# A transformer layer on one core: five engines leave one shared list of steps and each walk a table of its own

## The chip, the cores and the metric

The kernel runs on one core of one Trainium2 chip. The metric is the time of one execution on the device, in microseconds (us), the median of three runs. The core's engines run side by side, each through its own queue in order, and meet through semaphores: TensorE (PE; its weight loads are PEld), VectorE (DVE), ScalarE (ACT), GpSimd (POOL) and SyncE (SP), which here only starts DMAs. An instruction that waits holds everything behind it on its engine.

## The reference

The input is 16 sequences of 128 tokens with 256 channels. Three residual blocks follow each other, each fed by a layer norm:

```python
x = x + attn(layernorm(x))        # 16 heads with 72 latent dims, causal, keys = values = x @ latent_w + latent_b
x = x + birwkv(layernorm(x), ctx) # sigmoid(r) * (Af + Ab + e^(u+k) v) / (Bf + Bb + e^(u+k)); scans forwards and backwards in time
x = x + moe(layernorm(x))         # router over 8 experts, top 2, silu(x Wg) * (x Wu), then Wd, weighted sum
```

In the attention, q is projected per head, scores are masked and go through a softmax, the mixed latents of the 16 heads are projected by `out_w`. In the last block each token goes to its two best experts (512 hidden units each), and the two results are added with the router's weights.

## The kernel before, in words

**Steps.** The whole program is cut into named steps, such as `S.17` or `up.3.0`. One list, `STEPS`, completed by `schedule()` into `ORDER`, holds all of them. Each of the five engine programs walks that same list and does its own part of each step, or nothing. So a step can stand only at one place, and all its parts stand at that place in their engines' queues.

**Attention.** Work goes by 64 units; a unit is one sequence and four of its heads. A unit n has these steps: `S.n` (scores on PE, L743 and L750; row maximum on DVE, L1235; exponentials on ACT, L1011), `N.n` (reciprocal of the sums on DVE, L1239; the multiplication of the probabilities on POOL, L1633), `T.n` (transposition on PE, L758; copy on ACT, L1016) and `Y.n` (the product with the values on PE, L768; copy on DVE, L1250; the store by head for SP, L577). Two score banks and three probability buffers are used in turn, so `S.n` waits for the exponentials of unit n-2. The queries of two sequences are one group k: `q.k.i` projects them (PE), adds the bias (ACT, L1004) and SP moves them to another layout (L564, tile qT); unit 8k is the first to need them all. `O.b.i` projects the result of sequence b (PE, L796, and L781 for the last sequence); `add` adds it to x.

**Scans.** They lie beside the attention, for four groups g of four sequences and two channel halves k: `w1` to `w5` (DVE, L1264, L1274 and L1276 are the multiplication and the four scans), `w6`, `w7` and `wa` (POOL), `w8` (reciprocals on DVE, L1281) and `wb.g.k` (transposition on PE, L803; copy on ACT, L1044).

**Router and plan.** `x2`, `bn`, `agg`, `rs`, `nmb`, `xn`, `tx` (kind 3), `lg`, `r1` to `r4`, `ra` and `rw` choose experts and slots for a group of sequences; `lg` is L812, `r3` is L819 and L823 on PE, which waits for `r2` on DVE (L1344). `p1`, `p2` and `p3` (DVE, L1378 to L1473) plan which expert each tile of tokens takes: `p*.0` for the first five tiles after the third group, `p*.1` for the rest.

**Experts.** There are 23 tiles: 16 of 256 token slots with weights split in a high and a low part, then 7 of 128. Tile j has: `lw.j.k` (SP loads a third of its weights, 512 KB), `sw.j.k` (high part on ACT, L1076; low part on DVE, L1162), `ltk.j` (SP loads its token list, L635), `lxg.j` (POOL gathers its rows, L1690), `tg.j` (transposition on PE, L838; copies on ACT and DVE), `up.j.n`, `si`, `hd`, `sh` (gate and up products on PE, L672 or L872; silu and hidden values), `dn.j` (down product on PE, L672 or L881; weighting on ACT, L1105) and `ao.j` (POOL adds the rows into the output by an indirect DMA, L1717). `ao.j` waits until the adds of tile j-1 have landed, and the ACT part of `dn.j` waits for those of tile j-2. `gtk`, `gw` are the same loads for the first tiles, issued by POOL.

**Order.** What an engine does next is fixed by its place in `ORDER` alone. The waits are worked out from counts over `ORDER` and state what data or buffer must be ready.

## Time and profile before

| | us |
|---|---|
| median of 3 runs | 597.67 |
| lowest and highest | 597.42, 598.23 |
| span of the profiled execution | 602.4 |
| PE busy in it | 524.7 |
| DVE, ACT, POOL busy | 363.1, 329.2, 314.9 |

The profiled execution is 4.7 us longer than the median. A stretch in which PE is not busy, or busy at a granted clock below 1.00, is one in which the busiest engine does less than it could. "PEclk" is that clock as a share of 2.4 GHz; 0.50 is 1.2 GHz. Within the records, work that PE does for one step can hold a wait of its own between two matmul groups.

### The profile page before, as it was taken

The page shows a single profiled execution, that of the slowest core. Times are in us where ns is not written, and L with a number is a line of the kernel's source. Part 1 is how long each engine was busy: PE and PEld are TensorE (multiplying, and loading weights), DVE is VectorE, ACT ScalarE, POOL GpSimd, SP SyncE. Part 2 cuts the span into 40 slices and gives each one's busy share as a digit, 9 for nine tenths or more (in the row PEclk, how much of TensorE's full clock was granted, in tenths as well). Part 3 has the DMA queues.
Part 4 walks back from the last instruction along what each step waited for, and adds up shares of the span by engine and source line. Part 5 has one row for each costly group of instructions (what it writes and reads, how often), then busy time and mean ns, then how long its engine had stood idle before and what let it go on. Part 6 is the DMA issues. An engine that isn't in the chain of part 4 may idle for free.

```text
span 602.4 us, 10421 instructions
## 1 busy us (share of the span) xinstructions
PE 524.7 (87%) x3490; PEld 455.9 (76%) x3490; DVE 363.1 (60%) x749; ACT 329.2 (55%) x944; POOL 314.9 (52%) x277
## 2 busy tenths in 40 slices
...
PEclk9999999998999999999988879589999999999797
...
GB/s 189 166 3 123 58 65 101 57 72 87 57 96 102 65 59 66 105 77 70 64 26 91 111 140 226 124 96 83 280 154 287 210 238 228 235 253 358 176 27 0
DMA packets 53087, 75.65 MB, mean 126 GB/s; under 512 B 10185, under 2 KB 41674, under 8 KB 52778
## 3 DMA queue, kind: packets, MB, share of 16 engines
...
q10 hardware_dynamic: 888, 0.15, 0.1%
...
## 4 chain that ended last, share of the span: by engine, by line
PE 39%; DMA 22%; issue 12%; DVE 9%; POOL 9%; ACT 4%; SPq 3%; POOLq 1%; another core or an unknown queue 0%; ACTq 0%
DMA out<-Y,TK 14%; PE P L672 10%; PE PO L796 8%; PE P L750 6%; PE P L768 5%; DMA qT<-qP 3%; POOL out L1717 3%; PE P L758 3%; DMA zP<-ZT 2%; SPq L577 2%; POOL cxa L1690 2%; ACT EB L1011 2%; POOL xs L1676 1%; DMA arena<-wd 1%; PE P L743 1%
## 5 line engine op out<-in xcount | busy, mean ns | idle before, releaser
L1011 ACT ACTIVATE EB<-P,small 128x128 f32<-128x128 f32 x256 | 90.7, 369 | 79.3 <-DVE small L1235 60.1
L1633 POOL TENSOR_TENSOR EB<-EB,small 128x512 f32<-128x512 f32 x64 | 78.9, 1241 | 98.4 <-DVE small L1239 98.2
L672 PE MATMUL P<-GT,WF 128*128 128x256 f32 x768 | 100.8, 290 | 7.2 <-DVE GT L1162 2.6
L672 PEld LDWEIGHTS P<-GT,WF 128*128 128x128 f32 x768 | 96.4, 196 | 8.2 <-DVE GT L1162 3.1
L1717 POOL DMA_INDIRECT out<-Y,TK x39 | 67.4, 1729 | 66.3 <-DMA out<-Y,TK 28.9
L768 PE MATMUL P<-PT,V 128*72 128x512 f32 x128 | 68.7, 619 | 11.2 <-ACT PT L1016 10.1
L750 PEld LDWEIGHTS P<-KT,qT 72*128 72x128 f32 x512 | 67.7, 194 | 12.6 <-DMA qT<-qP 6.8
L750 PE MATMUL P<-KT,qT 72*128 72x128 f32 x512 | 68.9, 278 | 5.4 <-DMA qT<-qP 4.7
L796 PE MATMUL PO<-Ow,zP 128*128 128x256 f32 x270 | 71.2, 407 | 2.0 <-DMA zP<-ZT 1.9
L1250 DVE COPY ZT<-P 72x512 f32<-72x512 f32 x64 | 43.3, 677 | 45.1 <-PE P L768 42.1
L796 PEld LDWEIGHTS PO<-Ow,zP 128*128 128x128 f32 x270 | 52.9, 205 | 17.2 <-issue 10.7
L1235 DVE TENSOR_REDUCE small<-P 128x4 f32<-128x512 f32 x64 | 43.4, 678 | 27.1 <-PE P L750 25.6
L1016 ACT ACTIVATE PT<-P 128x512 f32<-128x512 f32 x64 | 38.8, 606 | 33.5 <-PE P L758 33.5
L1690 POOL DMA_INDIRECT cxa<-xd,TK x39 | 43.1, 1104 | 25.1 <-DMA TK<-xs 11.8
L672 PE MATMUL PO<-WF,HR 128*128 128x256 f32 x384 | 49.0, 284 | 4.8 <-issue 4.8
L1011 ACT ACTIVATION_READ_ACCUMULATOR EB<-P,small 128x1 f32 x256 | 52.9, 207 | 0.0
L1676 POOL DMA_INDIRECT xs<-TKS,SL x32 | 33.5, 1048 | 35.9 <-DVE TKS L1370 25.6
L672 PEld LDWEIGHTS PO<-WF,HR 128*128 128x128 f32 x384 | 47.1, 192 | 5.2 <-issue 5.2
L758 PEld LDWEIGHTS P<-ident,EB 128*128 128x128 f32 x256 | 31.6, 145 | 21.4 <-issue 11.4
L758 PE MATMUL P<-ident,EB 128*128 128x128 f32 x256 | 39.7, 278 | 3.3 <-POOL EB L1633 3.1
L1105 ACT ACTIVATE Y<-PO,TK 128x256 f32<-128x256 f32 x39 | 16.7, 470 | 45.6 <-DMA out<-Y,TK 25.4
L672 PE MATMUL P<-xnTa,Wd 128*128 128x256 f32 (+1 forms) x258 | 38.5, 303 | 2.7 <-ACT qP L1004 2.6
...
## 6 DMA issues: line engine op xcount, KB each, us to landing
...
```

The source lines that it names most:

```text
L672: r = e.matmul(o, lt(a), rt_(b), start=start and n == 0, stop=stop and n == 2, skip_group_check=skip)
L750: p = e.matmul(S[:, 128 * j:128 * j + 128], qT[k % 2][:, 4 * hq + j, c:c + 128], KT[g % 2][:, r:r + 128], start=False, stop=True, skip_gro ...
L758: p = e.transpose(PTB[:, 128 * j:128 * j + 128], EB[n % 3][:, j, :], ident[:, :])
L768: e.matmul(YB[0:L, :], V[g % 2][:, b % GB, :], PT[n % 2][:, :], start=True, stop=True).then_inc(s_Y, 1)
L796: p = e.matmul(o, zP[b // NB % 2][:, m, 128 * (b % NB):128 * (b % NB) + 128], Ow[:, m, :], start=m == 0, stop=m == NQ - 1)
L1011: e.activation(EB[i][:, j, :], S[:, 128 * j:128 * j + 128], ACT.Exp, bias=NM[i][:, j:j + 1], accum_out=SM[i][:, j:j + 1]).then_inc(s_exp, 1)
L1235: e.tensor_reduce(NM[n % 3], SB[n % 2][:, :].rearrange("p (h s) -> p h s", h=4), AX.X, ALU.max, negate=True).then_inc(s_max, 1)
L1250: e.tensor_copy(ZT[buf][:, :, c:c + 128], YB[0:L, :].rearrange("p (h t) -> p h t", h=4)).then_inc(s_z, 1)
L1633: e.tensor_tensor(EB[i][:, :, :], EB[i][:, :, :], SM[i].unsqueeze(2).broadcast_to([128, 4, 128]), ALU.mult).then_inc(s_prob, 1)
L1676: e.indirect_dma_start(xs, bass.IndirectOffsetOnAxis(ap=SL[:, g, c, b:b + 1], axis=0), TKS[:, g, c, b, :], None).then_inc(s_sc[g], 16)
L1690: e.indirect_dma_start(XG[i][:, a_, :], None, xd[0:(TN * 3 // 4, TN + 1)[phase(j)], :], bass.IndirectOffsetOnAxis(ap=TK[:, j, a_, 0:1].bit ...
L1717: e.indirect_dma_start(outr, bass.IndirectOffsetOnAxis(ap=TK[:, j, a_, 0:1].bitcast(i32), axis=0), Y[j % 2][:, a_, :], None, bounds_check= ...
```

## The change

Five tables stand beside `STEPS`: `SYNC_STEPS`, `TENSOR_STEPS`, `VECTOR_STEPS`, `SCALAR_STEPS` and `GPSIMD_STEPS`. Each engine's loop walks its own table. `ORDER` remains, and all waits are still worked out from it, so every step waits for the same events as before. Every step that has instructions on an engine is in that engine's table once. No instruction is added or removed.

```diff
+SYNC_STEPS = """
+    ctx.0 ctx.1 q.1.0 q.1.1 q.1.2 q.1.3 q.1.4 Y.1 Y.3 q.2.0 q.2.1 Y.5 Y.7 q.2.2 q.2.3 q.2.4 Y.9 ctx.2 q.3.0 q.3.1 Y.11 q.3.2 Y.13 Y.15 q.3.3 q.3.4
...
+def steps_of(table):
+
+    return [(name, *map(int, a)) for name, *a in (w.split(".") for w in table.split())]
...
-            for name, *a in ORDER:
+            for name, *a in steps_of(SYNC_STEPS):
...
-            for name, *a in ORDER:
+            for name, *a in steps_of(TENSOR_STEPS):
...
-            for s in ORDER:
+            for s in steps_of(GPSIMD_STEPS):
                 name, a = s[0], s[1:]
```

The order of the steps within one kind is kept on every engine, but for the weight parts `lw` and `sw` of neighbouring tiles. What moves is how the kinds interleave: on PE, the `q` come on average 4 steps earlier and the `Y` 2 steps later; on DVE the `w8` come on average 16 steps earlier; on SP the `ltk` 13 steps earlier and the `out` stores 12 later.

**Place 1, the end of the attention, DVE.** Lines of before are those of the profile; in the changed kernel all of them are 102 higher. L1402 to L1409 are `p3.0`; the reductions from P1 and P2 are the row maxima of units 62 and 63; the copies to ZT are `Y` steps. Before:

```order
L1235 TENSOR_REDUCE small<-P1 128x4
L1250 COPY ZT1<-P4 72x4x128
L1239 RECIPROCAL small<-small 128x4
L1402 TENSOR_TENSOR small<-small 1x40
L1403 TENSOR_TENSOR small<-small 1x40
L1404 TENSOR_REDUCE small<-small 1x5
L1405 SCALAR_TENSOR_TENSOR small<-small 1x5
L1406 TENSOR_SCALAR small<-small 1x5
L1407 TENSOR_TENSOR small<-small 1x5
L1408 TENSOR_TENSOR small<-small 1x5
L1409 CAST PI<-small 1x5
L1235 TENSOR_REDUCE small<-P2 128x4
```

After `p3.0` the maximum of unit 63 is next on DVE. Now:

```order
L1504 TENSOR_TENSOR small<-small 1x40
L1505 TENSOR_TENSOR small<-small 1x40
L1506 TENSOR_REDUCE small<-small 1x5
L1507 SCALAR_TENSOR_TENSOR small<-small 1x5
L1508 TENSOR_SCALAR small<-small 1x5
L1509 TENSOR_TENSOR small<-small 1x5
L1510 TENSOR_TENSOR small<-small 1x5
L1511 CAST PI<-small 1x5
L1352 COPY ZT1<-P4 72x4x128
L1337 TENSOR_REDUCE small<-P1 128x4
L1341 RECIPROCAL small<-small 128x4
L1352 COPY ZT0<-P4 72x4x128
```

Both maxima have moved behind `p3.0`: that of unit 62 stands between the `Y` copies of units 59 and 60, and that of unit 63 follows four rows below.

**The same place on PE.** L743 and L750 are `S`, L758 `T`, L768 `Y`, L796 and L781 `O`. Before:

```order
L743 MATMUL P2<-maskr,identr 128x512
L750 MATMUL P2<-KT1,qT1 128x128 x4
L768 MATMUL P4<-PT1,V1 72x512
L758 MATMUL P3<-ident,EB0 128x128 x4
L768 MATMUL P4<-PT0,V1 72x512
L796 MATMUL PO<-Ow,zP1 128x256 x3
L758 MATMUL P3<-ident,EB1 128x128 x4
L768 MATMUL P4<-PT1,V1 72x512
```

These are `S.63`, `Y.59`, `T.60`, `Y.60`, `O.14.0`, `T.61` and `Y.61`: the last scores stand ahead of `T.60`. Now (L860 is `T`, L870 `Y`, L898 `O`, L905 `wb`):

```order
L860 MATMUL P3<-ident,EB0 128x128 x4
L898 MATMUL PO<-Ow,zP0 128x256 x9
L870 MATMUL P4<-PT1,V1 72x512
L860 MATMUL P3<-ident,EB1 128x128 x4
L845 MATMUL P2<-maskr,identr 128x512
L852 MATMUL P2<-KT1,qT1 128x128 x4
L905 MATMUL PO<-ident,cu2 128x128 x4
L870 MATMUL P4<-PT0,V1 72x512
L860 MATMUL P3<-ident,EB2 128x128 x4
L870 MATMUL P4<-PT1,V1 72x512
```

`T.60` has moved ahead of `S.63`; the whole of `O.13` stands between `T.60` and `T.61`, and `wb.3.1` behind `S.63`.

**Place 2, the first expert tiles, PE.** `up.0.0` is the pair on P0 and P2, `up.0.1` the pair on P1 and P3; L819 and L823 are `r3.3`, L812 `lg.3`, L838 `tg`. Before:

```order
L672 MATMUL P0<-GT0,WF0 128x256 x12
L672 MATMUL P2<-GT0,WF0 128x256 x12
L690 MATMUL P5<-ident,XN 128x128 x4
L812 MATMUL P5<-small,XT3 128x8 x8
L819 MATMUL P5<-Mr,Utr 128x32
L823 MATMUL P5<-Mr,onem 128x8 x10
L672 MATMUL P1<-GT0,WF0 128x256 x12
L672 MATMUL P3<-GT0,WF0 128x256 x12
L838 MATMUL P4<-ident,cxa 128x128 x4
L672 MATMUL PO<-WF0,HR0 128x256 x24
L672 MATMUL P0<-GT1,WF1 128x256 x12
L672 MATMUL P2<-GT1,WF1 128x256 x12
```

`r3.3` stands ahead of `up.0.1`. Now (L914 is `lg`, L921 and L925 `r3`, L940 `tg`):

```order
L774 MATMUL P2<-GT0,WF0 128x256 x12
L792 MATMUL P5<-ident,XN 128x128 x2
L940 MATMUL P4<-ident,cxa 128x128 x4
L792 MATMUL P5<-ident,XN 128x128 x2
L914 MATMUL P5<-small,XT3 128x8 x8
L774 MATMUL P1<-GT0,WF0 128x256 x12
L774 MATMUL P3<-GT0,WF0 128x256 x12
L940 MATMUL P4<-ident,cxa 128x128 x4
L774 MATMUL P0<-GT1,WF1 128x256 x12
L774 MATMUL P2<-GT1,WF1 128x256 x12
L921 MATMUL P5<-Mr,Utr 128x32
L925 MATMUL P5<-Mr,onem 128x8 x10
```

`up.0.1`, `tg.2` and `up.1.0` have moved ahead of `r3.3`, and `tg.1` between the two transpositions.

**Place 3, the last expert tiles, POOL.** L1690 gathers rows (`lxg`), L1717 adds results (`ao`); the first rows here are `ao.12`. Before:

```order
L1717 DMA out<-Y0,TK 2048x256 x2
L1690 DMA cxa<-xd,TK 128x256
L1717 DMA out<-Y1,TK 2048x256 x2
L1690 DMA cxa<-xd,TK 128x256
L1717 DMA out<-Y0,TK 2048x256 x2
L1690 DMA cxa<-xd,TK 128x256
L1717 DMA out<-Y1,TK 2048x256 x2
L1690 DMA cxa<-xd,TK 128x256
L1717 DMA out<-Y0,TK 2048x256
L1690 DMA cxa<-xd,TK 128x256
```

Each gather stands behind the add of a tile five earlier. Now, from the same add (L1792 gathers, L1819 adds):

```order
L1819 DMA out<-Y0,TK 2048x256 x2
L1792 DMA cxa<-xd,TK 128x256 x3
L1819 DMA out<-Y1,TK 2048x256 x2
L1819 DMA out<-Y0,TK 2048x256 x2
L1819 DMA out<-Y1,TK 2048x256 x2
L1819 DMA out<-Y0,TK 2048x256
L1792 DMA cxa<-xd,TK 128x256 x3
L1819 DMA out<-Y1,TK 2048x256
```

The gathers of tiles 17, 18 and 19 stand in one row behind `ao.12`, and those of 20 to 22 behind `ao.16`.

## Rows read from the trace of the kernel before

**Rows 1.** The page: the granted TensorE clock in 40 slices of the span, in tenths.

```profile
PEclk9999999998999999999988879589999999999797
```

**Rows 2.** Busy time by stretch: length, PE, PEld, DVE, ACT, POOL, PEclk, DMA share, GB/s.

```profile
20.00:295.00 275.00, 260.79 (x1664) 215.09 (x1663) 191.23 (x390) 175.61 (x637) 153.87 (x129) 0.99 0.43 74
295.00:309.00 14.00, 12.03 (x50) 9.10 (x49) 7.99 (x22) 7.29 (x27) 7.63 (x7) 0.76 0.19 37
337.00:356.00 19.00, 12.09 (x31) 7.27 (x29) 8.53 (x26) 3.68 (x12) 10.42 (x14) 0.64 0.44 127
363.00:425.00 62.00, 45.93 (x306) 42.59 (x305) 39.45 (x112) 28.22 (x45) 24.51 (x20) 0.83 0.48 131
425.00:540.00 115.00, 111.42 (x932) 111.04 (x931) 82.20 (x101) 78.05 (x124) 66.06 (x46) 1.00 0.86 243
540.00:603.00 63.00, 45.00 (x324) 42.08 (x323) 5.40 (x8) 11.07 (x24) 25.75 (x18) 0.87 0.47 135
```

**Rows 3.** Timeline of PE: score products that wait for queries (units 24, 32, 56).

```profile
141.20 1.16 PE L750 MATMUL P<-KT,qT 72*128 72x128 f32 x8 [2.51 <-DMA qT<-qP]
...
180.55 1.16 PE L750 MATMUL P<-KT,qT 72*128 72x128 f32 x8 [1.27 <-DMA qT<-qP]
...
300.19 2.07 PE L750 MATMUL P<-KT,qT 72*128 72x128 f32 x8 [0.92 <-DMA qT<-qP]
```

**Rows 4.** Timelines of PE, DVE and ACT at the end of the attention.

```profile
342.91 1.98 PE L768 MATMUL P<-PT,V 128*72 128x512 f32 x2 [5.69 <-ACT PT L1016]
...
339.34 0.69 DVE L1235 TENSOR_REDUCE small<-P 128x4 f32<-128x512 f32 x1 [0.94 <-remote]
...
342.25 0.61 ACT L1016 ACTIVATE PT<-P 128x512 f32<-128x512 f32 x1
```

**Rows 5.** Timeline of PE from the first expert product on.

```profile
373.97 1.96 PE L672 MATMUL P<-GT,WF 128*128 128x256 f32 x12 [2.50 <-DVE WF L1162]
378.15 0.69 PE L690 MATMUL P<-ident,XN 128*128 128x128 f32 x2 [2.21 <-ACT XN L972]
...
387.47 0.40 PE L819 MATMUL P<-Mr,Utr 128*128 128x32 f32 x1 [3.42 <-DVE small L1344]
...
389.84 5.47 PE L672 MATMUL P<-GT,WF 128*128 128x256 f32 x24
...
400.53 3.04 PE L672 MATMUL P<-GT,WF 128*128 128x256 f32 x24
```

**Rows 6.** Timelines of POOL, ACT and PE among the expert tiles.

```profile
448.10 1.42 POOL L1690 DMA_INDIRECT cxa<-xd,TK  x1 [9.51 <-DMA TK<-xs]
...
463.28 0.84 ACT L1105 ACTIVATE Y<-PO,TK 128x256 f32<-128x256 f32 x2 [4.68 <-DMA out<-Y,TK]
...
465.47 3.11 PE L672 MATMUL PO<-WF,HR 128*128 128x256 f32 x24 [3.18 <-issue]
```

**Rows 7.** Timelines of POOL, then PE, in the last tiles.

```profile
555.91 1.01 POOL L1690 DMA_INDIRECT cxa<-xd,TK  x1 [0.75 <-DMA TK<-xs]
...
593.39 1.55 POOL L1717 DMA_INDIRECT out<-Y,TK  x1 [1.98 <-DMA out<-Y,TK]
...
562.01 0.69 PE L838 MATMUL P<-ident,cxa 128*128 128x128 f32 x2 [4.51 <-DMA cxa<-xd,TK]
562.49 3.62 PE L881 MATMUL PO<-arena,HS 128*128 128x256 f32 x8
...
570.23 1.89 PE L881 MATMUL PO<-WR,HS 128*128 128x256 f32 x8
```

**Rows 8.** POOL's multiplication: page (busy us, mean ns), its durations in ns, one with a scan.

```profile
L1633 POOL TENSOR_TENSOR EB<-EB,small 128x512 f32<-128x512 f32 x64 | 78.9, 1241 | 98.4 <-DVE small L1239 98.2
...
L1633 POOL TENSOR_TENSOR EB<-EB,small x64: 1030/1042/3067, 33.7 to 344.4; 128x512 f32<-128x512 f32 x64
...
54.77 3.00 POOL L1633 TENSOR_TENSOR EB<-EB,small 128x512 f32<-128x512 f32 x1 [7.49 <-DVE small L1239]
...
54.62 1.20 DVE L1274 TENSOR_TENSOR_SCAN arena<-D,arena 128x517 f32<-128x517 f32 x1
```

More of the change, by code:

```diff
@@ L182 @@
 """
+SYNC_STEPS = """
+    ctx.0 ctx.1 q.1.0 q.1.1 q.1.2 q.1.3 q.1.4 Y.1 Y.3 q.2.0 q.2.1 Y.5 Y.7 q.2.2 q.2.3 q.2.4 Y.9 ctx.2 q.3.0 q.3.1 Y.11 q.3.2 Y.13 Y.15 q.3.3 q.3.4
+    Y.17 Y.19 ctx.3 Y.21 Y.23 q.4.0 q.4.1 q.4.2 q.4.3 q.4.4 Y.25 q.5.0 xd.0.0.4 Y.27 Y.29 Y.31 q.5.1 q.5.2 q.5.3 q.5.4 Y.33 Y.35 Y.37 Y.39 q.6.0 q.6.1
+    q.6.2 q.6.3 q.6.4 Y.40 Y.41 Y.42 Y.43 out.0.0.4 out.1.0.4 q.7.0 q.7.1 Y.44 Y.45 Y.46 Y.47 q.7.2 q.7.3 q.7.4 xd.1.0.4 Y.48 Y.49 Y.50 Y.51 owh Y.52
+    Y.53 Y.54 Y.55 Y.56 Y.57 Y.58 Y.59 xd.2.0.4 ltk.3 lw.2.0 ltk.4 lw.1.0 lw.1.2 lw.1.1 xd.3.0.2 lw.2.1 xd.3.2.2 lw.3.0 lw.3.1 lw.4.0 lw.2.2 lw.3.2
+    lw.4.1 out.2.0.4 out.3.0.2 out.3.2.2 lw.5.0 lw.5.1 ltk.5 ltk.6 lw.4.2 lw.6.1 ltk.7 ltk.8 lw.6.0 ltk.9 ltk.10 lw.5.2 ltk.11 lw.7.1 lw.7.0 ltk.12
+    ltk.13 ltk.14 lw.6.2 ltk.15 ltk.16 ltk.17 lw.8.1 lw.8.0 ltk.18 lw.9.1 lw.9.0 lw.10.1 lw.7.2 lw.8.2 lw.10.0 ltk.19 lw.11.0 lw.11.1 lw.9.2 lw.10.2
+    lw.12.0 lw.12.1 lw.13.1 lw.13.0 lw.11.2 lw.12.2 lw.14.0 lw.14.1 lw.13.2 lw.15.0 lw.15.1 lw.17.0 lw.14.2 lw.16.0 lw.15.2 ltk.20 lw.16.2 lw.18.0
+    lw.17.1 lw.16.1 lw.17.2 ltk.21 lw.18.1 lw.19.1 lw.20.1 lw.19.0 lw.20.0 lw.18.2 lw.19.2 lw.20.2 lw.21.1 lw.21.2 ltk.22 lw.22.1 lw.22.2 lw.21.0
+    lw.22.0
@@ new lines @@
+"""
+GPSIMD_STEPS = """
+    rs.1.0.0.4 qd.0 rs.1.1.0.4 w6.0.0 w7.0.0 N.0 N.1 N.2 wa.0.0 w6.0.1 N.3 w7.0.1 rs.1.2.0.4 N.4 N.5 N.6 N.7 N.8 wa.0.1 w6.1.0 N.9 w7.1.0 N.10 N.11
+    xb.2 wa.1.0 N.12 N.13 N.14 w6.1.1 xb.3 xb.0 xb.1 xb.4 w7.1.1 N.15 N.16 N.17 wa.1.1 N.18 w6.2.0 N.19 N.20 w7.2.0 N.21 N.22 wa.2.0 N.23 N.24 N.25
+    rs.1.3.0.4 w6.2.1 N.26 N.27 rs.2.0.0.4 w7.2.1 wa.2.1 x2.0.0.0.0 x2.0.0.2.0 N.28 rs.3.0.0.4 N.29 w6.3.0 N.30 N.31 N.32 N.33 N.34 w7.3.0 N.35 N.36
+    N.37 N.38 N.39 N.40 N.41 wa.3.0 w6.3.1 N.42 N.43 rs.2.1.0.4 N.44 x2.1.0.0.0 x2.1.0.2.0 N.45 N.46 r4.0.0.4.0.0 r4.0.0.4.0.2 rs.3.1.0.4 w7.3.1 N.47
+    N.48 N.49 N.50 N.51 r4.0.0.4.1.0 wa.3.1 xb.5 N.52 rs.2.2.0.4 N.53 N.54 x2.2.0.0.0 N.55 x2.2.0.2.0 N.56 N.57 rs.3.2.0.4 xb.6 r4.0.0.4.1.2
+    r4.1.0.4.0.0 N.58 r4.1.0.4.0.2 r4.1.0.4.1.0 r4.1.0.4.1.2 N.59 N.60 N.61 r4.2.0.4.0.0 r4.2.0.4.0.2 r4.2.0.4.1.0 r4.2.0.4.1.2 N.62 gtk.0 gtk.1
+    gw.0.0 rs.2.3.0.2 N.63 gw.0.1 lxg.0 gw.0.2 gtk.2 rs.3.3.0.2 xb.7 rs.2.3.2.2 lxg.1 rs.3.3.2.2 lxg.2 lxg.3 lxg.4 r4.3.0.4.0.0 r4.3.0.4.0.2
+    r4.3.0.4.1.0 r4.3.0.4.1.2 ao.0 lxg.5 lxg.6 ao.1 lxg.7 ao.2 lxg.8 lxg.9 lxg.10 ao.3 ao.4 lxg.11 lxg.12 ao.5 lxg.13 ao.6 lxg.14 lxg.15 ao.7 lxg.16
+    ao.8 ao.9 ao.10 ao.11 ao.12 lxg.17 lxg.18 lxg.19 ao.13 ao.14 ao.15 ao.16 lxg.20 lxg.21 lxg.22 ao.17 ao.18 ao.19 ao.20 ao.21 ao.22
@@ L185, in schedule @@
+"""
+def steps_of(table):
+    return [(name, *map(int, a)) for name, *a in (w.split(".") for w in table.split())]
 def schedule():
-    order = [(name, *map(int, a)) for name, *a in (w.split(".") for w in STEPS.split())]
+    order = steps_of(STEPS)
     def emit(*step):
@@ L1105, in weigh @@
                     e.activation(Y[j % 2][:, a_, :], PO[:, j % 2, C * a_:C * a_ + C], ACT.Copy, scale=TK[:, j, a_, 1:2]).then_inc(s_y, 1)
-            for name, *a in ORDER:
+            for name, *a in steps_of(SCALAR_STEPS):
                 if name == "consts":
@@ L1506, in hidden_lo @@
                 sub_lo(r[:, 1], HF[n][:, :].rearrange("p (f t) -> p f t", f=2), r[:, 0]).then_inc(s_hrlo, 1)
-            for s in ORDER:
+            for s in steps_of(VECTOR_STEPS):
                 name, a = s[0], s[1:]
```

69 lines of the change are left out of this document (added).

## The prediction

> **What bounds the kernel now.** I read the page first [rows 1], then the busy time by stretch [rows 2], then the timelines where a stretch loses much. The span is 602.4 us. TensorE (PE) is the busiest engine, and its granted clock falls below 9 tenths in nine slices of 40: one near 135 us, three from 300 to 345, then 346, 376 and 391, and two behind 555 [rows 1]. So two losses add up: time in which PE is idle, and time in which it works at 1.2 instead of 2.4 GHz. By stretch [rows 2], idle is length minus busy, and the clock's part is estimated as busy times (1 - PEclk):
> - 20 to 295 us, the attention: idle 275.0 - 260.8 = 14.2, clock 2.6, together 16.8. PE is saturated here but for small gaps.
> - 295 to 309: 2.0 + 2.9 = 4.9.
> - 337 to 356, the end of the attention: 6.9 + 4.4 = 11.3.
> - 363 to 425, router and first expert tiles: 16.1 + 7.8 = 23.9.
> - 425 to 540, expert tiles: 3.6. Saturated.
> - 540 to 603, last tiles and end: 18.0 + 5.9 = 23.9.
>
> No work is added or removed, so the change can only win or lose in these sums. What lies outside them is work that PE must do anyway.
>
> **The change part by part.** (a) *Attention, 20 to 295.* Two score products wait inside for the queries that SP moves: 2.51 us for unit 24 and 1.27 us for unit 32 [rows 3]. In PE's table, the last `q` step of group 3 now stands 7 steps further ahead of the unit that needs it, and the store `out.0`, which shared the DMA queues with group 4's queries, is 22 steps later on SP. Take the 3.8 us as removed, and 1.2 more for idle time near them. Against it, PE takes the scan transpositions `wb.1.0` and `wb.1.1` 17 and 12 steps earlier. If the product that they need is late, all of PE waits. The trace shows no such wait, so its price is bounded: below by zero, above by the third rival. I put 5 us of new waits against the 5 gained and count nothing here.
>
> (b) *Unit 56.* Its scores wait 0.92 us for queries and run 2.07 us where those of unit 24 take 1.16 [rows 3]. The whole stretch from 295 to 309 loses 4.9 [rows 2]. The three last `q` steps of group 7 move 14 to 19 steps forward on PE, 8 to 10 on ScalarE (ACT), and the last of them 4 on SP. What is late next is the ordinary chain of scores, maximum and exponentials of two units earlier. Credit 3.5, at most 4.9, at least 0.
>
> (c) *End of the attention.* PE idles 5.69 us for the copy of unit 60 [rows 4]. That copy comes last in a chain which is one of order, not of data: DVE does the plan `p3.0` first and takes the maximum of unit 63 at 339.34, ACT's exponentials of unit 63 follow, and only then comes the copy of unit 60 at 342.25 [rows 4]. PE had handed over its input when the idle began, at 342.91 - 5.69 = 337.2. In the new tables ACT copies units 60, 61 and 62 before those exponentials, and `O.13` stands on PE behind `T.60`. I laid both queues out with the trace's durations: `T.62` is then the step that comes late, by about 1 us. The clock should then not fall, as it did behind the 5.69. Credit 8.5 of 11.3.
>
> The Trainium skill, TensorE: Matmul & The Clock Gate, section "HAM oscillation — how this bites in real kernels", says that idle gaps which make the clock fall cost twice, once as the gap and once as slow work behind it. By that rule the trace agrees (5.47 us for what takes 3.04, [rows 5]), and a stall that the new order makes would also cost more than its own length.
>
> (d) *Router and first tiles.* In [rows 5] the second half of `up.0.0` waits 2.50 for weights, the next transposition 2.21 for the norm, and `r3` 3.42 for DVE's choices; `up.0.1` stands behind `r3` and runs 5.47 us where the same work takes 3.04 at the full clock. New: `sw.0.1` is ahead of the norm's shift on DVE, `up.0.1`, `tg.2` and `up.1.0` are ahead of `r3`, and DVE fills its wait for the logits with weight splits. I laid the new order out by hand with the trace's durations, from the last attention products to the end of `up.3.1`. Before, that is the stretch of 62 us in [rows 2]; then it is about 52, with some 5 us of idle left ahead of the logits. Credit 7.5 of 10.
>
> (e) *Token lists.* POOL stands 9.51 us for the token list of tile 8 [rows 6] with the add of tile 3 queued behind it. That add lands late, ACT stands 4.68 for it at 463.28, and PE 3.18 at 465.47 [rows 6]. SP now loads that list 5 steps earlier, behind the lists of tiles 5 to 7. Credit 3.0.
>
> (f) *Last tiles.* The gather of tile 19 stands behind the add of tile 14 until 555.91, PE idles 4.51 for it, and the next product takes 3.62 where 1.89 is usual [rows 7]: 6.2 us. The gathers of 17 to 19 are now ahead of the add of tile 13. But the adds form a chain of their own, each waiting for the one before to land; the last starts at 593.39, behind a DMA [rows 7]. It is shorter only if (e) lets it keep up. Credit 3.5.
>
> Head (0 to 20) and last add to end are untouched. Sum: 3.5 + 8.5 + 7.5 + 3.0 + 3.5 = 26.0 us. 602.4 - 26.0 = 576.4 in a profiled execution; the one profiled was 4.7 above the median, so **571.7 us**.
>
> **The rivals.** *1. VectorE's scans hold the probabilities.* POOL's multiplication takes 1.04 us as a rule and 3.07 at most [rows 8]. The one at 54.77 takes 3.00 and starts 0.15 behind a scan [rows 8], with another scan queued behind that. Over 64 of them the excess is 78.9 - 64 x 1.04 = 12 us (78.9 is that line's busy time, [rows 8]). The new DVE table puts three scans of a half in a row more often (`w2`, `w3`, `w4`). Should that double the excess, with every added us on the path: 571.7 + 12 = 584. For it: DVE and POOL are busy for 191 and 154 of the 275 us of the attention [rows 2]. Against it: most multiplications have slack, since only some transpositions wait for them.
>
> The Trainium skill, SBUF — State Buffer, section "SBUF: two separate sides", states that the port pair of VectorE and GpSimd is an exclusive lock, held for a whole instruction. The long row agrees; by the rule a run of three scans could hold one multiplication for longer still.
>
> *2. The experts gain nothing.* If the DMAs bound the chain of adds (their share is 0.86 from 425 to 540, [rows 2]), then (e) and (f) only move slack. 571.7 + 6.5 = 578. SP's table also puts seven token lists ahead of weights for tile 8, which could eat more.
>
> *3. Slower: PE stands at the scan transpositions.* Each of the eight `wb` needs a chain over DVE, ACT and POOL, and PE's order is fixed. If the product is late by one unit at each, that is 275 / 64 = 4.3 us, eight times, 34 us: 571.7 + 34 = 606. It decides from 26 / 8 = 3.3 us per `wb` on. For it: `wb` moved more than most steps. Against it: the same tables move POOL's `w6`, `w7`, `wa` 5 to 8 steps and DVE's `w8` 16 steps forward, so the chain is moved with it.
>
> *4. It does nothing.* If the waits alone set the real order, the losses stay: 597.7. Against it, (c) and (f) are waits of order and not of data.
>
> **How the numbers follow.** Forecast 0.62 (571.7, own range 557 to 584, from full credits to half of them), rival 1 0.12, rival 2 0.11, rival 3 0.11, rival 4 0.04. A measurement can tell about 0.2% from no change. Faster: 0.62 + 0.12 + 0.11 = 0.85; same 0.04; slower 0.11. Full credits in (b) to (f) and in (a) without new waits are 41 us at the most (557); the upper end, 597, takes in rivals 1 and 2 and a mild form of 3.
>
> **What would show it.** Right, if in the changed profile the idle of PE for the copy of unit 60 is under 2 us and the clock stays at 9 tenths from 337 to 356; if `r3` does not hold PE; if POOL's wait for a token list is gone and the gather of tile 19 lands before PE needs it. Wrong, if PE waits several us at the scan transpositions (L803 before), if its idle time in the attention rises above 14 us, if multiplications of over 2 us become many, or if PE is done with the last tile early and the adds are not.

## The result, and the profile after

| | before | changed |
|---|---|---|
| median, us (4 runs each) | 597.54 | 613.26 |
| lowest, highest | 596.63, 598.23 | 611.77, 618.11 |
| span of the profiled execution | 602.4 | 612.3 |
| PE busy in it | 524.7 | 529.0 |

The changed kernel is slower: ratio 1.0265, 95% interval 1.0217 to 1.0313. Every ratio, here and below, leaves out the slow executions, those over 1.5% above the fastest of their kernel. The two spans differ by 9.9 us and the medians by 15.7: the profiled span of before is 4.7 us above its median, that of the changed kernel 1.0 below.

The page of the changed kernel, the granted clock in 40 slices, against [rows 1]:

```profile
PEclk9999996999997999999899978699999979989787
```

From 306 to 352 us there is no low slice any more, where three stood before. New ones stand at 92 to 107 and at 184 to 199 us, in the attention, and at 490 to 505 among the expert tiles, where the kernel before had slices of 9 tenths; one of 8 tenths is new at 291 to 306. Busy time by stretch, as in [rows 2]:

```profile
20.00:295.00 275.00, 253.41 (x1587) 209.66 (x1585) 186.63 (x360) 169.65 (x610) 138.50 (x113) 0.96 0.41 67
...
337.00:366.00 29.00, 23.82 (x106) 16.92 (x105) 17.74 (x59) 10.22 (x35) 18.57 (x21) 0.88 0.24 68
366.00:425.00 59.00, 52.64 (x357) 49.81 (x358) 48.24 (x127) 34.31 (x52) 33.41 (x28) 0.88 0.67 189
...
480.00:540.00 60.00, 51.28 (x406) 50.60 (x405) 35.20 (x43) 32.55 (x53) 29.08 (x19) 0.94 0.77 218
540.00:612.00 72.00, 52.22 (x364) 48.58 (x362) 8.44 (x12) 13.45 (x29) 27.17 (x20) 0.86 0.44 117
```

The attention now idles 275.0 - 253.4 = 21.6 us where it was 14.2, with the clock at 0.96 instead of 0.99. By the sum of the forecast (idle, and busy times 1 - PEclk) that stretch loses 21.6 + 10.1 = 31.7 us instead of 16.8, so 14.9 more. Among the expert tiles, from 480 to 540, PE idles 8.7 us where the kernel before was saturated (its own row for that stretch has PE busy 60.00 of 60.00).

To see where time goes I set both timelines side by side and took, step by step, when PE ends it, changed minus before. All such differences are to one profiled execution of before.

| PE ends | before, us | changed minus before |
|---|---|---|
| scores of unit 32 | 181.7 | +7.0 |
| scores of unit 56 | 302.3 | +7.5 |
| scores of unit 63 | 335.9 | +13.7 |
| transposition of unit 63 | 358.6 | +5.8 |
| up product of tile 3 | 424.9 | -4.2 |
| down product of tile 8 | 486.7 | -6.6 |
| down product of tile 22, the last | 590.2 | +11.8 |

A step that has itself moved in PE's table, as the scores of units 56 and 63 have, is not a mark of equal work. So I also counted the columns that PE's matmuls have put out and compared the times at which both kernels have done the same amount. Where the kernel before stands at 295 us, the changed one is 13.8 us behind; at 309 it is 11.5, at 337 it is 12.4, at 358.6 it is 5.8, at 486.7 it is 6.8 ahead, at 540 it is 6.3 behind, and at 590.2 it is 11.8 behind.

The last add ends 9.9 us later. So the attention costs 5.8 net (about 14 lost up to 295, and 6.6 won back at its end), router and first tiles win back 10.0, tiles 4 to 8 win 2.4, and from tile 8 on 18.4 go. That last stretch is the finding: it was forecast partly as untouched and partly as a gain.

**What PE waits for in the attention** (timelines of PE, ACT and SP; [rows 3] are those of before):

```profile
97.15 2.08 PE L852 MATMUL P<-KT,qT 72*128 72x128 f32 x8 [6.08 <-DMA qT<-qP]
...
186.60 2.07 PE L852 MATMUL P<-KT,qT 72*128 72x128 f32 x8 [4.91 <-DMA qT<-qP]
...
186.64 0.84 ACT L1106 ACTIVATE qP<-P,small 128x256 f32<-128x256 f32 x2 [9.36 <-DMA qT<-qP]
...
155.88 9.49 SPq L679 DMA_DIRECT2D zP<-ZT  x8
165.47 5.90 SPq L666 DMA_DIRECT2D qT<-qP  x9
```

Units 16 and 32 wait 6.08 and 4.91 us for queries. ACT had the first queries of unit 32 ready at 145.5, but SP has the stores of units 19, 21 and 23 ahead of them: all nine transfers start in one bunch at 165.47 and end in one bunch at 186.6. ACT, whose next queries need the same buffer, stands there for 9.36 us. Up to 337 us PE's waits for queries go from 4.7 to 12.1 us in all, those for DVE's `Y` copies from 1.0 to 5.1. The score rows show the price behind: the long score rows take 2.07 us for what takes 1.05 at the full clock.

**What waits among the expert tiles** (timelines of ACT, DVE and PE at tile 12):

```profile
487.50 0.84 ACT L1207 ACTIVATE Y<-PO,TK 128x256 f32<-128x256 f32 x2 [6.31 <-DMA out<-Y,TK]
...
489.81 0.69 DVE L1603 TENSOR_TENSOR HF<-SG,P 128x512 f32<-128x512 f32 x1 [5.36 <-ACT SG L1192]
...
491.24 1.09 PE L940 MATMUL P<-ident,cxa 128*128 128x128 f32 x4 [5.33 <-DVE GT L1264]
```

Read it downwards: ACT weights the result of tile 8, which needs a Y buffer that is free only when the adds of tile 6 have landed. The silu of tile 10 stands behind that on ACT, the hidden values of tile 10 and then the row copy of tile 11 behind the silu on DVE, and PE behind DVE. The new PE table brings this about: it runs down products in pairs (tiles 7 and 8, 10 and 11, 13 and 14, 15 and 16, 17 and 18), 3.4 us apart for the first pair, where the old one has one every 9.1 us. There are two Y buffers, and an add waits for the one before: from tile 9 to tile 13 the adds start 10.8, 10.1, 10.3 and 11.2 us apart. That the waits run along this chain is read from the rows; that it is the pairs that bring them about is argued, since no run takes the pairs apart on PE.

**The last tiles** (timelines of ACT, POOL and PE; against [rows 7]):

```profile
536.41 0.84 ACT L1207 ACTIVATE Y<-PO,TK 128x256 f32<-128x256 f32 x2 [4.81 <-DMA out<-Y,TK]
...
572.84 0.47 ACT L1207 ACTIVATE Y<-PO,TK 128x256 f32<-128x256 f32 x1 [6.20 <-DMA out<-Y,TK]
...
573.27 1.55 POOL L1819 DMA_INDIRECT out<-Y,TK  x1 [2.97 <-DMA out<-Y,TK]
575.13 1.01 POOL L1792 DMA_INDIRECT cxa<-xd,TK  x1 [0.30 <-issue]
...
578.74 0.69 PE L940 MATMUL P<-ident,cxa 128*128 128x128 f32 x2 [6.42 <-DMA cxa<-xd,TK]
```

The gather that was late in [rows 7], of tile 19, is early now; the gather of tile 20 stands behind the add of tile 16 instead and costs PE 6.42.

### The profile page after: what moved, and what is told of

It reads as the page before. It is cut to its first block, busy times and chain, and to the rows that moved or that the text cites. A ratio compares the mean times of both kernels' runs of the same rounds, so it can differ in the third digit from the quotient of the medians.

```text
span 612.3 us, 10456 instructions
## 1 busy us (share of the span) xinstructions
PE 529.0 (86%) x3490; PEld 461.4 (75%) x3490; DVE 370.0 (60%) x749; ACT 331.2 (54%) x946; POOL 322.9 (53%) x277
## 4 chain that ended last, share of the span: by engine, by line
PE 34%; DMA 25%; POOL 11%; DVE 10%; issue 9%; ACT 5%; SPq 4%; POOLq 1%; ACTq 0%; DVEq 0%
DMA out<-Y,TK 14%; PE P L774 9%; DMA qT<-qP 6%; PE P L852 6%; PE PO L898 5%; PE P L870 4%; POOL out L1819 3%; PE P L860 3%; PE P L974 2%; POOL EB L1735 2%; SPq L666 2%; ACT EB L1113 2%; POOL xs L1778 1%; PE PO L983 1%; PE P L845 1%
## 5 line engine op out<-in xcount | busy, mean ns | idle before, releaser
L1735 POOL TENSOR_TENSOR EB<-EB,small 128x512 f32<-128x512 f32 x64 | 74.5, 1176 | 108.7 <-DVE small L1341 108.6
L1819 POOL DMA_INDIRECT out<-Y,TK x39 | 68.3, 1750 | 79.0 <-ACT Y L1207 50.1
L774 PEld LDWEIGHTS P<-GT,WF 128*128 128x128 f32 x768 | 98.1, 201 | 6.0 <-DVE GT L1264 5.3
L852 PEld LDWEIGHTS P<-KT,qT 72*128 72x128 f32 x512 | 69.2, 198 | 19.4 <-DMA qT<-qP 13.4
L852 PE MATMUL P<-KT,qT 72*128 72x128 f32 x512 | 70.6, 282 | 12.5 <-DMA qT<-qP 12.1
L870 PE MATMUL P<-PT,V 128*72 128x512 f32 x128 | 68.9, 620 | 7.4 <-DVE ZT L1352 7.2
L898 PE MATMUL PO<-Ow,zP 128*128 128x256 f32 x270 | 65.7, 389 | 0.0
L898 PEld LDWEIGHTS PO<-Ow,zP 128*128 128x128 f32 x270 | 51.0, 197 | 9.8 <-issue 3.8
L1113 ACT ACTIVATION_READ_ACCUMULATOR EB<-P,small 128x1 f32 x256 | 55.2, 216 | 0.0
L774 PE MATMUL PO<-WF,HR 128*128 128x256 f32 x384 | 51.1, 292 | 1.5 <-issue 1.4
L1792 POOL DMA_INDIRECT cxa<-xd,TK x39 | 44.5, 1142 | 13.5 <-issue 9.5
L860 PEld LDWEIGHTS P<-ident,EB 128*128 128x128 f32 x256 | 31.9, 148 | 25.8 <-POOL EB L1735 14.6
L774 PEld LDWEIGHTS PO<-WF,HR 128*128 128x128 f32 x384 | 48.9, 199 | 2.1 <-issue 2.1
L860 PE MATMUL P<-ident,EB 128*128 128x128 f32 x256 | 41.0, 285 | 9.0 <-POOL EB L1735 8.1
L1106 ACT ACTIVATE qP<-P,small 128x256 f32<-128x256 f32 x63 | 26.9, 475 | 33.4 <-DMA qT<-qP 17.5
L1778 POOL DMA_INDIRECT xs<-TKS,SL x32 | 32.8, 1026 | 21.6 <-DVE TKS L1472 12.7
```

Of the source, the lines that this page charges most:

```text
L774: r = e.matmul(o, lt(a), rt_(b), start=start and n == 0, stop=stop and n == 2, skip_group_check=skip)
L852: p = e.matmul(S[:, 128 * j:128 * j + 128], qT[k % 2][:, 4 * hq + j, c:c + 128], KT[g % 2][:, r:r + 128], start=False, stop=True, skip_gro ...
L860: p = e.transpose(PTB[:, 128 * j:128 * j + 128], EB[n % 3][:, j, :], ident[:, :])
L870: e.matmul(YB[0:L, :], V[g % 2][:, b % GB, :], PT[n % 2][:, :], start=True, stop=True).then_inc(s_Y, 1)
L898: p = e.matmul(o, zP[b // NB % 2][:, m, 128 * (b % NB):128 * (b % NB) + 128], Ow[:, m, :], start=m == 0, stop=m == NQ - 1)
L1113: e.activation(EB[i][:, j, :], S[:, 128 * j:128 * j + 128], ACT.Exp, bias=NM[i][:, j:j + 1], accum_out=SM[i][:, j:j + 1]).then_inc(s_exp, 1)
```

## The experiments

Names: "old" and "new" are the orders of the kernel before and of the changed one. A step list cut at a step X means that on each engine all steps ahead of X in `ORDER` stand first, the rest behind. Ratios are to the kernel before on the same chip; the experiments ran on four chips, so ratios and not times are to be compared across groups. Differences on PE are to the profile of before, and each comes from one execution. Kernels that have the old order up to unit 56 are between 4.2 us ahead and 1.0 behind there, before their first changed step, so a lead of a few us in a profile is no gain yet. The table after the last experiment collects the one number that I read from each profile.

**One engine's table at a time.** sp_only is the kernel before with SP's new table; sp_old is the changed kernel with SP on the old one.

```diff
# sp_only: the four other engines
-            for name, *a in steps_of(TENSOR_STEPS):
+            for name, *a in ORDER:
# sp_old: SyncE
-            for name, *a in steps_of(SYNC_STEPS):
+            for name, *a in ORDER:
```

The edit is shown in short: in both kernels the engines' loops still walk their tables, and the old order is written out in the table itself. In sp_old, two token lists (tiles 15 and 16) stand one place ahead of their place in `ORDER`.

> The kernel before, but SyncE walks the new table. Theory A: the queries of units 32 to 39 are issued in one bunch behind four copies, TensorE waits for them at unit 32 and behind, 603 to 607 us. Rival D: within 1 us of the kernel before, 597 to 599 us.

> The changed kernel, but SyncE walks the old table (two of its token list loads one place earlier). Theory A: the queries of units 32 to 39 go out 10 to 20 us earlier, TensorE's wait of 4.9 us at unit 32 goes and its clock stays at 1.00 there; the end is 605 to 608 us. Rival D (the order of TensorE and ScalarE is what loses, SyncE only follows): 612 to 614 us.

Measured: 652.1 us (ratio 1.098, 1.091 to 1.106) and 694.9 (1.170, 1.162 to 1.177). Neither theory had this. SP's table is not a fault that can be taken out: an engine's table fits the order of the others, and I take it that with a foreign one SP stands at its head while what others need is ready behind it. In sp_only its wait for ACT's queries goes from 58.9 us to 129.9; in sp_old its wait for DVE's `Y` copies is 131.6 (82.8 in the changed kernel). These runs say nothing on which table loses time in the changed kernel, and after them I cut only by place, on all engines at once, or moved single steps.

**Cut at the first expert tile.**

```diff
# TENSOR_STEPS of split_attn, around the cut; the other tables likewise
-    O.15.2 O.15.3 tg.0 tx.3.3.0.2.0 tx.3.3.0.2.1 up.0.0 tx.3.3.2.2.0 tg.1
+    O.15.2 O.15.3 tx.3.3.0.2.0 tx.3.3.0.2.1 tg.0 up.0.0 tx.3.3.2.2.0 tx.3.3.2.2.1 lg.3.0.4.0 lg.3.0.4.2 r3.3.0.4 up.0.1 tg.1
```

> On every engine the new tables up to the first expert tile (its gather, its steps tg.0 and all behind it walk the old order). Theory A (the new order loses in attention because SyncE's table holds queries behind mixed-value copies, and it loses again among the experts because the adds into the output, one behind another, set the end): attention ends about 6 us late as in the changed kernel and the old experts add nothing of their own, 603 to 605 us. Rival B (all loss is in the experts' order, attention's late end is made good by the slack of the router): 597 to 599 us. Rival C (all loss is in attention): 611 to 614 us.

> The complement: the old order up to the first expert tile, the new tables behind it. Theory A: TensorE gains the 10 us of the router as in the changed kernel, loses them by the chain of adds and by the output copies that stand ahead of gate work on ScalarE, and ends 4 us late, 600 to 604 us. Rival B (experts' order alone is the loss, and all of it): 611 to 614 us. Rival C (experts' order is a gain that attention's lateness ate): 586 to 590 us.

Measured: split_attn 608.9 (1.022, 1.016 to 1.029), split_exp 611.2 (1.028, 1.021 to 1.036). Either half alone costs nearly the whole 2.65%, so the halves don't add up; that time lost in the attention is hidden in the experts' own loss is my reading, not a measurement. In split_exp PE is 11.8 us ahead at tile 8 and 9.9 behind at the end. Both times are above theory A (603 to 605 and 600 to 604): it named both places of the loss and priced them too low. The profiled span of split_attn is only 5.8 us above [rows 2]'s 602.4, but its ratio says 13 us, since that profile of before is long. Rival C falls with split_exp; B has the time of split_exp right, but falls with split_attn.

**Cut the adds.** The same adds, each behind the one before, with 16 rows instead of 128 (the other rows are left out of the output).

```diff
-                    e.indirect_dma_start(outr, bass.IndirectOffsetOnAxis(ap=TK[:, j, a_, 0:1].bitcast(i32), axis=0), Y[j % 2][:, a_, :], None,
+                    e.indirect_dma_start(outr, bass.IndirectOffsetOnAxis(ap=TK[0:16, j, a_, 0:1].bitcast(i32), axis=0), Y[j % 2][0:16, a_, :], None,
```

> The kernel before, but each add into the output takes 16 rows in place of 128 (its output leaves the others out); the same number of adds, each behind the one before. Rival F for the adds (the chain of adds sets the end): each of the 23 tiles' adds is shorter by 2 us or more from tile 8 on, 580 us or less. Theory E (the adds run beside TensorE and are only felt in the last tile): 594 to 598 us.

> split_exp (old attention, new experts) with the adds cut to 16 rows. The new table puts output copies, which wait for an add to land, ahead of the gates of later tiles on ScalarE. If it is by the landing of the adds that the new order loses, the loss goes with them: 585 to 595 us against the 611 of split_exp. If it loses by something else: 607 to 611 us.

Measured: 597.7 (0.995, 0.990 to 1.000) and 591.4 (0.988, 0.980 to 0.996). The old order hardly feels its adds; split_exp takes 4% less with the short ones, and then beats the kernel before. Tile 12's rows on PE in adds16_exp, and POOL's line for the adds there and in split_exp (count, busy us, mean ns, idle ahead):

```profile
481.45 0.63 PE L938 MATMUL P<-ident,cxa 128*128 128x128 f32 x4
```

```profile
L1817 POOL DMA_INDIRECT out<-Y,TK x39 | 56.9, 1459 | 71.3 <-DMA out<-Y,TK 38.0 <-ACT Y L1205 24.4 <-issue 8.9
```

```profile
L1817 POOL DMA_INDIRECT out<-Y,TK x39 | 66.2, 1697 | 83.3 <-ACT Y L1205 58.2 <-DMA out<-Y,TK 14.6 <-issue 10.5
```

In split_exp the same row on PE had waited 5.66 us. So the loss behind tile 8 comes through the adds, and in the new order only. This is the pair that I would keep if I could keep only one.

**New order in the middle only.** new_router: new from tile 0 to tile 7. new_mid60: new from unit 60 to tile 7. new_end: new from unit 60 to the end of the attention. Old elsewhere.

```diff
# TENSOR_STEPS of new_mid60, against the changed kernel, behind tile 7
-    up.9.0 up.9.1 dn.7 tg.11 dn.8 up.10.0 up.10.1 tg.12 dn.9 up.11.0 up.11.1 up.12.0 up.12.1 dn.10 tg.13 dn.11
+    dn.7 up.9.0 up.9.1 tg.10 dn.8 up.10.0 tg.11 up.10.1 dn.9 up.11.0 tg.12 up.11.1 dn.10 up.12.0 tg.13 up.12.1 dn.11
```

> On every engine the new order only for the steps from the first expert tile's to tile 7's (the router's last part among them), the old order ahead and behind. In split_exp this stretch had TensorE 12 us ahead at tile 8. Theory E (the loss sits in three places of the new order behind tile 8, and the old order there keeps what it is given): 585 to 589 us. Rival F (the stage behind tile 8 is bound by the adds into the output or by the DMA engines, which have no room for 12 us): 593 to 598 us.

> As new_router, but the new order begins at attention unit 60, so that the end of attention (forecast term c) is in it. If the end of attention gains on its own, this ends 3 to 8 us below new_router; if the 8 us that TensorE made up there in the changed kernel were only slack of its own lateness, within 1.5 us of new_router.

> The new order from unit 60 to the end of attention only, the old one ahead and behind: forecast term c alone. In new_mid60 TensorE was 11 us ahead at the last unit. If this lead is carried to the end: 587 to 590 us on a chip where the kernel before takes 597. If the old router and first tiles absorb it (they wait for the router, the token lists and the adds, not for TensorE): 594 to 598 us.

Measured: new_router 597.4, the median of eleven executions from 587 to 604 (the ratio of 0.983, 0.976 to 0.990, rests on two of them, so I don't lean on it; the median itself is rival F's number), new_mid60 591.0 (0.988, 0.979 to 0.996), new_end 594.0 (0.987, 0.978 to 0.995). In new_end PE is 9.0 us ahead at the last unit and 8.3 at the end; in new_mid60 22.6 ahead at tile 3, 15.8 at tile 6, and 15.6 at the end. So in the profiles both gains come, and the old order behind tile 8 keeps what it is given. By ratio the end of the attention alone is a gain; what router and first tiles add to it is not told apart by new_mid60 (0.988 against new_end's 0.987). 6 us go between tiles 4 and 6, at the last rows of this (timelines of POOL, ACT and PE in new_mid60):

```profile
430.18 1.92 POOL L1790 DMA_INDIRECT cxa<-xd,TK  x1 [0.30 <-issue]
432.40 1.42 POOL L1790 DMA_INDIRECT cxa<-xd,TK  x1 [0.30 <-issue]
434.12 2.54 POOL L1817 DMA_INDIRECT out<-Y,TK  x1 [0.30 <-issue]
...
445.77 0.84 ACT L1205 ACTIVATE Y<-PO,TK 128x256 f32<-128x256 f32 x2 [8.20 <-DMA out<-Y,TK]
...
448.44 4.38 PE L772 MATMUL PO<-WF,HR 128*128 128x256 f32 x24 [7.70 <-issue]
```

The new POOL table has six gathers (tiles 8, 9, 10) ahead of the add of tile 3. They delay that add, the add delays ACT's copy of tile 5, and the copy PE's next down product by 7.70.

**Single steps moved.** exp_act and exp_pool start from split_exp, attn_q from split_attn.

```diff
# exp_act, SCALAR_STEPS
-    sh.9.1 dn.8 sw.10.2 si.10.0 si.10.1 sw.12.0 sw.12.1 tg.12 sh.10.0
+    sh.9.1 sw.10.2 si.10.0 si.10.1 sw.12.0 sw.12.1 tg.12 dn.8 sh.10.0
...
-    sh.14.0 sh.14.1 dn.13 sw.15.2 tg.15
+    sh.14.0 sh.14.1 sw.15.2 tg.15 dn.13
# exp_pool, GPSIMD_STEPS
-    ao.13 ao.14 ao.15 ao.16 lxg.20 lxg.21 lxg.22 ao.17
+    ao.13 ao.14 lxg.20 ao.15 lxg.21 ao.16 lxg.22 ao.17
# attn_q, SYNC_STEPS
-    Y.17 Y.19 ctx.3 Y.21 Y.23 q.4.0 q.4.1 q.4.2 q.4.3 q.4.4
+    Y.17 q.4.0 Y.19 ctx.3 Y.21 q.4.1 q.4.2 Y.23 q.4.3 q.4.4
```

> split_exp with two output copies of ScalarE moved: tile 8's from ahead of the gates of tile 10 to behind the gathered rows of tile 12, tile 13's from ahead of the rows of tile 15 to behind them. Theory G (the copy waits for an add to land, and what stands behind it on ScalarE keeps TensorE waiting): the two waits of 5.7 and 3.0 us at tiles 12 and 15 go, TensorE at tile 10 is 5 us earlier than in split_exp, the end 603 to 607 us. Rival H (the chain of adds itself sets the end, TensorE's waits are only its reflection): the waits go or move, but the adds of tiles 13 to 22 stand where they stood, 609 to 612 us.

> split_exp with the gathers of tiles 20, 21, 22 on GpSimd ahead of the adds of tiles 15, 16, 17 in place of all three behind the add of tile 16. If the last tiles lose by the late gather: TensorE's wait of 6.5 us at tile 20 goes, 604 to 607 us. If the adds, one behind another, hold the last tiles anyway: 609 to 612 us.

> split_attn (new attention, old experts) with three steps of SyncE moved: the queries q.4.0 ahead of the mixed values of unit 19, q.4.1 and q.4.2 ahead of those of unit 23. Theory A: TensorE's wait of 4.9 us at unit 32 and ScalarE's of 9.4 us for the same queries go, TensorE is at unit 36 5 us or more ahead of split_attn, 602 to 605 us against 608.9. Rival D (TensorE's and ScalarE's own order loses there): within 1.5 us of split_attn.

Measured: exp_act 602.2 (1.003, 0.999 to 1.007), exp_pool 596.4 (0.998, 0.993 to 1.002), attn_q 607.3 (1.012, 1.003 to 1.020). Against split_exp's 1.028 the first two gain 2.5 and 3.1%, or 15 and 18 us, more than their waits (by times, from another chip, 9 and 15). But in exp_pool PE is already 7.5 us better at tile 10, five tiles ahead of the first moved step, because this execution's adds landed sooner: ACT's copy of tile 8, 6.65 us late in split_exp, waits

```profile
476.58 0.84 ACT L1205 ACTIVATE Y<-PO,TK 128x256 f32<-128x256 f32 x2 [0.42 <-DMA out<-Y,TK]
```

So that gain is not the edit's alone, and the profiled execution is the quickest of its kernel (593.2, of 593.2 to 602.5). attn_q is clean: SP's queries of unit 32 now go out as they become ready, and PE's scores of unit 32 wait for nothing (timelines of SP, PE):

```profile
145.40 1.30 SPq L664 DMA_DIRECT2D qT<-qP  x2
...
158.65 3.37 SPq L664 DMA_DIRECT2D qT<-qP  x4
...
182.06 1.05 PE L850 MATMUL P<-KT,qT 72*128 72x128 f32 x8
```

PE ends the scores of unit 36 at +3.3 instead of +11.7, and the last transposition at -1.8 instead of +5.1. But from there to tile 4 it falls back to +3.9, and at the last down product only 1.3 us of the profile's gain are left. By ratio it is 1.0% (6 us), with intervals that overlap: 1.003 to 1.020 against 1.016 to 1.029. Why the old router and first tiles take more time behind the repaired attention I have not settled. The wait of unit 16 (4.62 us here) is not repaired by any run.

**The repairs in the changed kernel itself,** alone and all three together, and late_repaired: old to unit 60, new behind, with the repairs on ACT and POOL. The edits are those shown.

> The changed kernel with the gathers of tiles 20, 21, 22 ahead of the adds of tiles 15, 16, 17. If the gain of exp_pool was the repair's: ratio to the kernel before 1.00 or less (600 us or less where the kernel before takes 600). If most of it was that chip's quicker adds: only the wait of 6.5 us at tile 20 goes, ratio 1.013 to 1.02.

> The changed kernel with the output copies of tiles 8 and 13 moved behind the rows of tiles 12 and 15 on ScalarE. If exp_act's 9 us were the repair's: ratio 1.005 to 1.015. If they were the chip's: the waits move to the next copy, ratio 1.02 to 1.03.

> The changed kernel with the three repairs together (the queries of attn_q on SyncE, the copies on ScalarE, the gathers on GpSimd). If the three places are independent and are the loss: 3 (queries) and 6 (gather) and 8 (copies) us off, ratio 0.985 to 1.0. If they hide one another behind the chain of adds: ratio 1.005 to 1.015.

> The old order to unit 60, the new one behind it, with the repairs on ScalarE and GpSimd. TensorE was 16 to 22 us ahead among the first tiles in new_mid60. If the repaired new order keeps what it is given, as the old one did: ratio 0.970 to 0.980, less than new_mid60's 0.988. If it still loses behind tile 8: 0.985 to 1.0.

Measured, all four on one chip: after_pool 611.3 (1.033, 1.022 to 1.045), after_act 610.1 (1.023, 1.009 to 1.037), after_three 608.0 (1.023, 1.014 to 1.032), late_repaired 592.0 (0.994, 0.990 to 0.998). In place of the gains of exp_pool and exp_act there is nothing outside the intervals. after_pool lies above both of its expectations and after_three above both of its own. In after_three ACT still waits 36.6 us for adds (31.2 in the changed kernel), in after_act 15.4, and neither is quicker for it. So two moved steps do not repair the loss; I take it to be spread over the new order behind tile 8.

**The version that is faster.** mid60_five is new_mid60 executed more often; mid60_pool has in addition one step moved.

```diff
# mid60_pool, GPSIMD_STEPS
-    ao.1 lxg.7 ao.2 lxg.8 lxg.9 lxg.10 ao.3 ao.4
+    ao.1 lxg.7 ao.2 lxg.8 ao.3 lxg.9 lxg.10 ao.4
```

> new_mid60 again, in more rounds, beside mid60_pool. The lead of 15 us that its profile showed at the end: ratio to the kernel before 0.975 to 0.985. The earlier timing: 0.979 to 0.996.

> new_mid60 with the add of tile 3 ahead of the gathers of tiles 9 and 10 on GpSimd instead of behind them. If the gathers (four of 1.0 to 1.9 us) hold that add and through its landing the output copy of tile 5 and TensorE: the add goes out 4.5 us earlier, TensorE's wait of 7.7 us ahead of tile 6's down product falls to about 3, the end 4 to 5 us below mid60_five. If the landing of the add sets it whenever it is issued: within 1 us of mid60_five.

Measured: mid60_five 590.4 (0.981, 0.974 to 0.989), mid60_pool 583.0 (0.976, 0.971 to 0.981). In mid60_pool the add of tile 3 goes out at 428.08 and ACT's copy of tile 5 waits for nothing:

```profile
428.08 1.62 POOL L1817 DMA_INDIRECT out<-Y,TK  x1 [0.35 <-issue]
...
437.81 0.83 ACT L1205 ACTIVATE Y<-PO,TK 128x256 f32<-128x256 f32 x2
```

PE is 24.2 us ahead at tile 3, 23.8 at tile 8 and 24.1 at the end. But 4.2 of that stand there at unit 56, ahead of the first changed step, this is the quickest of six executions, and the profile of before is a long one; by ratio the kernel gains 14 us. By medians it is 7.4 us below mid60_five, of which 4 to 5 were expected, but the two intervals overlap: the wait is gone, its price in time is not sure. This kernel beats both, the kernel before and the changed one.

**Time that PE loses from tile 8's down product to the last one,** against the kernel before, read from each profile (negative: gained):

| behind tile 8 | kernels | us |
|---|---|---|
| old order | split_attn, attn_q, new_end, new_router, new_mid60, mid60_five, mid60_pool | 0.5, -0.4, 0.0, 1.6, 0.2, 0.6, -0.3 |
| new order | changed kernel, split_exp, exp_act, exp_pool | 18.4, 21.7, 13.3, 0.6 |
| new order | after_pool, after_act, after_three, late_repaired | 9.5, 9.1, 10.2, 7.0 |
| adds of 16 rows | adds16_old, adds16_exp | -2.7, -3.7 |

The old order passes any lead on. The new one takes 7 to 22 us of it in seven of eight profiles. With the short adds the two orders are alike. How much it takes is not set by the pace of landing alone: the two profiles with the slowest adds (5.9 and 5.5 us from issue to landing, tiles 8 to 13) lose most, 21.7 and 18.4, but exp_act loses 13.3 with 4.1 and exp_pool 0.6 with 4.4. The profiles of exp_pool and after_pool are of the quickest execution of each, so their 0.6 and 9.5 are low ends.

## Why the prediction was wrong, point by point

The forecast was 576.4 us for a profiled execution and 571.7 for the median; it came to 612.3 and 613.3. By its own steps, against the table of step ends and the marks of equal work:

- **(a) Attention, no gain: wrong, 13.8 us lost up to 295 at equal work (+7.5 at the scores of unit 56, a step that has moved).** The waits of units 24 and 32 in [rows 3] were to go. That of unit 24 did. That of unit 32 grew from 1.27 to 4.91, and unit 16 got one of 6.08. I read the moves of `q` on PE and of one store on SP, and did not lay out SP's queue between them, where the stores of three units stand ahead of all five query steps of the group. attn_q shows this cause for unit 32: 8.4 us at unit 36. The rest, unit 16's wait among it, is untested. The 5 us set against it were put at the scan transpositions, where nothing waits (page of that line in the changed kernel, no entry under its waits):

```profile
L905 PE MATMUL PO<-ident,cu x16: 270/272/274, 85.6 to 349.8; 128*128 128x128 f32 x16
its engine sat idle before it (us, times) until:
who waited for it (us, times):
```

- **(b) Unit 56, 3.5: mis-sized.** Its wait for queries is gone, but between the scores of units 52 and 56 only 1.1 us are won, and from 295 to 309 at equal work 2.3.
- **(c) End of the attention, 8.5: right in kind, some 5 to 8 measured.** 6.6 from 337 to 358.6 at equal work in the changed kernel; 8.3 at the end when it is all that is changed (new_end), and 7.8 by its ratio, whose interval allows 2.7 to 13. The profile of before is a costly one here: five other kernels with the old order up to there (split_exp, exp_act, exp_pool, adds16_old, new_router) end unit 63's transposition 1.2 to 3.7 us earlier. After the same wait for the copy of unit 60, 5.73 us in exp_pool, the clock comes back sooner there, 0.82 where [rows 2] has 0.64:

```profile
337.00:356.00 19.00, 12.59 (x46) 8.21 (x47) 8.60 (x26) 5.71 (x15) 11.56 (x15) 0.82 0.45 131
```

In the changed kernel the idle time for the copy of unit 60 is gone. `T.62`, put down as late by about 1 us, waits 3.29 for POOL's multiplication, and the clock does not stay up: the slice from 352 to 367 us has 7 tenths, and the product behind takes 1.91:

```profile
354.17 1.11 PE L860 MATMUL P<-ident,EB 128*128 128x128 f32 x4 [3.29 <-POOL EB L1735]
355.08 1.91 PE L870 MATMUL P<-PT,V 128*72 128x512 f32 x2
```

- **(d) Router and first tiles, 7.5: right in kind, 10.0 measured.** `r3` stands behind `up.1.0` and waits for nothing, and the expert products ahead of the norm still wait as forecast (compare [rows 5]):

```profile
376.55 4.63 PE L774 MATMUL P<-GT,WF 128*128 128x256 f32 x24 [1.82 <-DVE GT L1264]
383.75 0.69 PE L792 MATMUL P<-ident,XN 128*128 128x128 f32 x2 [2.57 <-ACT XN L1074]
...
397.75 0.18 PE L921 MATMUL P<-Mr,Utr 128*128 128x32 f32 x1
```

- **(e) Token lists, 3.0: right, 2.4 measured on PE between tiles 3 and 8.** POOL's wait of 9.51 us in [rows 6] is gone:

```profile
440.95 1.02 POOL L1792 DMA_INDIRECT cxa<-xd,TK  x1 [0.30 <-DMA TK<-xs]
```

- **(f) Last tiles, 3.5, and the stretch before them, which got no term: this is the step that failed, 18.4 us lost on PE from tile 8 on, 16.5 at the last add.** At equal work 13.1 of it go between 486.7 and 540 and 5.5 behind 540, where the 3.5 were to be won. I took the stretch from 425 to 540 as saturated and untouched, since PE was busy all the time [rows 2]. That was a property of the old order, not of the work. I had written that the adds form a chain of their own and had looked at it for the last tile only. ACT's copy of tile j waits for the adds of tile j-2, and in the new tables that puts the chain in the way of silu and row copies from tile 8 on; with adds of 16 rows the loss is gone (21.7 us in split_exp, -3.7 in adds16_exp). That the down products in pairs do it is argued. The gather of tile 19 does land in time, as forecast, but that of tile 20 costs PE 6.42 in its place. Rival 2 named the adds but priced them as a gain not made (6.5 us), not as a loss.

The rivals: 1 is false as put, POOL's multiplication is busy 74.5 us against the 78.9 of [rows 8], with a mean of 1176 ns; but PE's waits for it rose from 3.1 to 8.1 us.

```profile
L1735 POOL TENSOR_TENSOR EB<-EB,small 128x512 f32<-128x512 f32 x64 | 74.5, 1176 | 108.7 <-DVE small L1341 108.6
```

Rival 3 had the right sign by a wrong mechanism, and 606 us near the 613.3 is luck: no `wb` waited. Rival 4 is excluded. The sentence on what would prove the forecast wrong did name "idle time in the attention above 14 us", which came (21.6).

The rule of the Trainium skill, TensorE: Matmul & The Clock Gate, section "HAM oscillation — how this bites in real kernels", that gaps which make the clock fall cost twice, is borne out again: behind the wait of 4.91 at unit 32 the scores take 2.07 where 1.05 is what they take in attn_q without it. The other one cited, of the exclusive port pair, decided nothing here.

Terms (c) and (d) were worked out well: 16.0 us together, and the kernel that has the new order only for them, with one POOL step repaired, gains 14 us by its ratio (583 us; the wait of (e) for the list of tile 8 is gone there too). A profiled execution of it has a span of 578.2, near the 576.4 of the sum: but the sum had counted (b) and (f) as well and set (a) at nothing, so this nearness is luck.
